# First attention: the mask moves from TensorE to VectorE, and the softmax subtraction from VectorE to GpSimd

## The reference

```python
xn = (x - mu) * jax.lax.rsqrt(var + LN_EPS) * ln_gamma + ln_beta
q = xn @ Wq
kv = context @ Wkv
dots = jnp.einsum('bhnd,bhmd->bhnm', q, k) * scale
dots = jnp.where(mask, dots, -jnp.inf)
attn = jax.nn.softmax(dots, axis=-1)
out = jnp.einsum('bhnm,bhmd->bhnd', attn, v)
return out @ Wo + bo
```

## Time and profile before

| | us |
|---|---|
| median of three runs | 2427.84 |
| span of the profiled execution | 2424.7 |
| TensorE busy | 2252.3 (93%) |
| VectorE busy | 1825.4 (75%) |
| ScalarE busy | 1492.7 (62%) |
| GpSimd busy | 517.2 (21%) |

### The profile page before, as it was taken

The page is one execution under the profiler, slowest core; times in us unless marked ns, Lnnn a source line. Parts: engine busy times, 40 slices in busy tenths (PEclk is TensorE's granted clock), DMA queues, the critical chain, the costliest instruction groups (busy, mean ns, idle before and its releaser), DMA issues.

```text
span 2424.7 us, 49203 instructions
## 1 busy us (share of the span) xinstructions
PE 2252.3 (93%) x14859; PEld 1942.3 (80%) x14861; DVE 1825.4 (75%) x4361; ACT 1492.7 (62%) x3090; POOL 517.2 (21%) x734
## 2 busy tenths in 40 slices
PE   7899999999899899995468999999997999979998
PEld 6788888888788788883147888888886788879998
DVE  3677777787966688887984877888878666865666
ACT  6455555556454677776886666666663654637666
POOL 2022221322212122121001111111101442421334
PEclk8999999999999999998579999999999999979999
DMA  8444544445300444440015455555452000115455
GB/s 216 115 129 127 141 132 135 131 122 145 95 16 8 127 128 128 135 125 27 0 37 152 135 142 149 144 138 144 131 139 72 1 1 1 39 41 146 140 141 159
DMA packets 461643, 256.56 MB, mean 106 GB/s; under 512 B 25664, under 2 KB 442332, under 8 KB 461532
## 3 DMA queue, kind: packets, MB, share of 16 engines
q1 hardware_dynamic: 461532, 255.27, 38.1%
HBM read 150.10 MB, written 105.12 MB: 105 GB/s over the span
## 4 chain that ended last, share of the span: by engine, by line
PE 79%; DVE 9%; ACT 5%; issue 4%; ACTq 0%; DMA 0%; POOL 0%; DVEq 0%; POOLq 0%
PE ps_o L906 13%; PE ps_s L890 12%; PE ps_p L87 7%; PE ps_p L89 7%; PE ps_p L88 7%; PE ps_t L879 6%; PE ps_o L1415 3%; PE ps_t L1415 2%; PE ps_s L3052 2%; PE ps_t L3070 2%; PE ps_o L3070 2%; PE ps_s L87 2%; PE ps_s L88 1%; PE ps_s L89 1%; DVE f_rng L1879 1%
## 5 line engine op out<-in xcount | busy, mean ns | idle before, releaser
L906 PEld LDWEIGHTS ps_o<-a_val,a_pt 128*128 128x128 f32 (+2 forms) x3200 | 412.5, 192 | 33.5 <-issue 7.6
L890 PE MATMUL ps_s<-a_keys,a_zt 128*128 128x308 f32 (+1 forms) x1024 | 416.8, 491 | 15.7 <-ACT a_keys L1025 9.8
L906 PE MATMUL ps_o<-a_val,a_pt 128*128 128x128 f32 (+2 forms) x3200 | 423.0, 275 | 5.3 <-ACT a_pt L1062 3.6
L1171 DVE TENSOR_REDUCE a_sm<-a_e 128x16 f32<-128x1232 f32 (+1 forms) x192 | 234.4, 1221 | 230.4 <-ACT a_e L1070 230.0
L1034 ACT ACTIVATE a_stage<-ps_p 128x512 f32<-128x512 f32 (+1 forms) x370 | 220.9, 597 | 287.7 <-PE ps_p L89 285.5
L1025 ACT ACTIVATE a_keys<-ps_p 128x308 f32<-128x308 f32 x603 | 257.5, 427 | 102.8 <-PE ps_p L89 102.3
L1062 ACT ACTIVATE a_pt<-ps_t 128x512 f32<-128x512 f32 (+1 forms) x448 | 225.3, 505 | 150.3 <-PE ps_t L879 149.9
L1156 DVE TENSOR_REDUCE a_mx<-ps_s 128x6 f32<-128x462 f32 (+1 forms) x512 | 256.5, 549 | 45.6 <-PE ps_s L890 28.5
L879 PE MATMUL ps_t<-ident,a_e 128*128 128x128 f32 (+1 forms) x1600 | 262.0, 276 | 28.1 <-DVE a_e L1179 25.8
L87 PE MATMUL ps_p<-ct_hi,a_mt_hi 96*128 (+1 forms) x603 | 258.9, 429 | 0.0
L1164 DVE TENSOR_TENSOR a_e<-ps_s,a_mx 128x462 f32<-128x462 f32 (+1 forms) x512 | 253.9, 546 | 0.0
(11 more groups left out here) (436 smaller groups left out, 4602.8 us busy)
## 6 DMA issues: line engine op xcount, KB each, us to landing
a_vals<-a_stage SPq DMA_DIRECT2D x160, 512.0 KB, 3.5
a_val<-a_vals SPq DMA_DIRECT2D x128, 576.0 KB
f_w<-in_L_ffn_W_dram SPq DMA_DIRECT2D x129, 256.0 KB, 2.7
a_vals<-a_stage SPq DMA_DIRECT2D x40, 416.0 KB
a_val<-a_vals SPq DMA_DIRECT2D x64, 256.0 KB
a_val<-a_vals SPq DMA_DIRECT2D x128, 40.0 KB
x<-in_x_dram SPq DMA_DIRECT2D x8, 512.0 KB, 7.0
out_dram<-x SPq DMA_DIRECT2D x7, 512.0 KB, 6.1
```

What stands on the lines that cost most here:

```text
L890: mm = eng.matmul(o, zt, keys[:, h0:h0 + nh, :], start=True, stop=not self.masked)
L906: mm = eng.matmul(c.ps_o[:, (i % 2) * P:(i % 2 + 1) * P], self.pt[0:r, n, :], self.val[0:r, i % 2, n, :], start=(n == 0), stop=(n == self. ...
L1171: eng.tensor_reduce(self.sm[:, :], e, AX.X, ALU.add).then_inc(st.sem, 1)
```

## The change

- TensorE no longer multiplies the mask in: 192 matmuls (three per tile) go, as does the rounded identity. Its wait for a free score bank is now on `scores_masked`.
- VectorE empties each score bank by adding the mask on the way to SBUF, and then takes the maxima from SBUF, in the order add 0, add 1, max 0, add 2, max 1, max 2. `mask_add` shrinks to one copy of 77 columns that the addition repeats over the heads. In the `found` iterations add 0 and max 0 come before `normalise`.
- GpSimd subtracts the maxima, bank by bank, SBUF to SBUF, and signals `shifted`. `mx` gets two halves.
- GpSimd's other work of this phase is reordered behind the subtractions: per iteration first the three subtractions of tile t+2, then, by position in the group, the bias addition, `next_stats.pool`, or the window copies and `ln.pool`. The window copies lose their wait for `probs_ready`.

```diff
     def scores(self, eng, t, b, zt, keys, first=False):
-            eng.wait_ge(self.shifted.sem, self.shifted.at(self.NB * (t - 1) + b + 1))
-        mm = eng.matmul(o, zt, keys[:, h0:h0 + nh, :], start=True, stop=not self.masked)
-        if self.masked:
-            mask = self.mask_add[:, 0:nh, :].rearrange("p h k -> p (h k)")
-            mm = eng.matmul(o, self.ident_r[:, :], mask, start=False, stop=True)
-        mm.then_inc(self.scores_ready.sem, 1)
+            eng.wait_ge(self.scores_read.sem, self.scores_read.at(self.NB * (t - 1) + b + 1))
+        eng.matmul(c.ps_s[:, b, 0:nh * KEYS], zt, keys[:, h0:h0 + nh, :], start=True, stop=True)\
+           .then_inc(self.scores_ready.sem, 1)
...
+    def masked_maxima(self, eng, t, par, banks):
+        def maximum(b):
+            heads, _, dest = self.bank_of(t, par, b)
+            eng.wait_ge(self.scores_masked.sem, self.scores_masked.at(self.NB * t + b + 1))
+            eng.tensor_reduce(self.mx[:, par, heads], dest, AX.X, ALU.max).then_inc(self.max_ready.sem, 1)
+        for b in banks:
+            _, src, dest = self.bank_of(t, par, b)
+            mask = self.mask_add[:, :].unsqueeze(1).broadcast_to([P, self.banks[b], KEYS])
+            eng.wait_ge(self.scores_ready.sem, self.scores_ready.at(self.NB * t + b + 1))
+            eng.tensor_tensor(dest, src, mask, ALU.add).then_inc(self.scores_masked.sem, 1)
+            if b - 1 in banks:
+                maximum(b - 1)
+        if banks:
+            maximum(banks[-1])
...
     def shift(self, eng, t, par, found=0):
+        if self.masked:
+            self.masked_maxima(eng, t, par, range(found, self.NB))
+            return
...
+    def shift_masked(self, eng, t, par):
+        for b in range(self.NB):
+            heads, _, dest = self.bank_of(t, par, b)
+            eng.wait_ge(self.max_ready.sem, self.max_ready.at(self.NB * t + b + 1))
+            eng.tensor_tensor(dest, dest, bc(self.mx[:, par, heads], KEYS), ALU.subtract)\
+               .then_inc(self.shifted.sem, 1)
...
+    def gpsimd_masked(self, eng, v_last):
+        self.shift_masked(eng, 0, 0)
+        self.shift_masked(eng, 1, 1)
+        for t in range(BATCH):
+            g, k = t // GT, t % GT
+            if t + 2 < BATCH:
+                self.shift_masked(eng, t + 2, k % 2)
+            if k == 1 and g + 1 < GROUPS:
+                self.ln.pool_bias(eng, g + 1)
+            elif k == 2 and g >= 1:
+                self.next_stats.pool(eng, g - 1)
+            elif k == 3:
+                w = t // self.WIN
+                if g % 2 == 1 and w + 2 < self.WINDOWS:
+                    eng.wait_ge(self.proj_done.sem, self.proj_done.at(self.use(w, v_last) + 1))
+                    self.copy_window(eng, w + 2)
+                if g + 2 < GROUPS:
+                    self.ln.pool(eng, g + 2)
+        self.next_stats.pool(eng, GROUPS - 1)
```

More of the change, by code:

```diff
@@ L631, in __init__ @@
             self.mask_u8 = sb(ctx, n("mask_u8"), [P, KEYS], mybir.dt.uint8)
-            self.mask_add = sb(ctx, n("mask_add"), [P, self.banks[0], KEYS], F32R)
-            self.ident_r = sb(ctx, n("ident_r"), [P, P], F32R)
+            self.mask_add = sb(ctx, n("mask_add"), [P, KEYS], F32)
             self.some_key = sb(ctx, n("some_key"), [P, 2], F32)
@@ L638, in __init__ @@
         self.val = sb(ctx, n("val"), [P, 2, self.chunks, P], F32)
-        self.mx = sb(ctx, n("mx"), [P, H], F32)
+        self.mx = sb(ctx, n("mx"), [P, 2, H], F32)
         self.sm = sb(ctx, n("sm"), [P, H], F32)
@@ L672, in __init__ @@
         self.lo_done = cl("split_lo", 4 * self.pairs)
-        self.mask_ready = cl("mask_ready", 5) if self.masked else None
+        self.mask_ready = cl("mask_ready", 4) if self.masked else None
         self.ln = TailLayerNorm(core, known, self.bias) if known else LayerNorm(core, twice, self.bias)
@@ L688, in __init__ @@
         self.shifted = cl("shifted", self.NB * T)
+        self.scores_masked = cl("scores_masked", self.NB * T) if self.masked else None
+        self.scores_read = self.scores_masked if self.masked else self.shifted
         self.exp_ready = cl("exp_ready", T)
@@ L971, in tensor @@
         eng.wait_ge(self.proj_copied.sem, self.proj_copied.at(self.first))
-        if self.masked:
-            eng.wait_ge(self.mask_ready.sem, self.mask_ready.at(5))
         for k in range(2):
@@ L1155, in maxima @@
             eng.wait_ge(self.scores_ready.sem, self.scores_ready.at(self.NB * t + b + 1))
-            eng.tensor_reduce(self.mx[:, heads], src, AX.X, ALU.max).then_inc(self.max_ready.sem, 1)
+            eng.tensor_reduce(self.mx[:, par, heads], src, AX.X, ALU.max).then_inc(self.max_ready.sem, 1)
+    def masked_maxima(self, eng, t, par, banks):
[12 more added lines that the diff above has]
+            maximum(banks[-1])
     def shift(self, eng, t, par, found=0):
+        if self.masked:
+            self.masked_maxima(eng, t, par, range(found, self.NB))
+            return
         self.maxima(eng, t, par, range(found, self.NB))
@@ L1163, in shift @@
             eng.wait_ge(self.max_ready.sem, self.max_ready.at(self.NB * t + b + 1))
-            eng.tensor_tensor(dest, src, bc(self.mx[:, heads], KEYS), ALU.subtract).then_inc(self.shifted.sem, 1)
+            eng.tensor_tensor(dest, src, bc(self.mx[:, par, heads], KEYS), ALU.subtract)\
+               .then_inc(self.shifted.sem, 1)
[4 more added lines that the diff above has]
+            eng.tensor_tensor(dest, dest, bc(self.mx[:, par, heads], KEYS), ALU.subtract)\
+               .then_inc(self.shifted.sem, 1)
     def normalise(self, eng, t, par):
@@ L1204, in vector @@
             m = self.mask_ready
-            for h in range(self.banks[0]):
-                ins = eng.tensor_scalar(self.mask_add[:, h, :], self.mask_u8[:, :], -1.0, 1e30, ALU.add, ALU.mult)
-            ins.then_inc(m.sem, 1)
+            eng.tensor_scalar(self.mask_add[:, :], self.mask_u8[:, :], -1.0, 1e30, ALU.add, ALU.mult)\
+               .then_inc(m.sem, 1)
             eng.tensor_reduce(self.some_key[:, 0:1], self.mask_u8[:, :], AX.X, ALU.add).then_inc(m.sem, 1)
@@ L1213, in vector @@
                .then_inc(m.sem, 1)
-            eng.tensor_copy(self.ident_r[:, :], c.ident[:, :]).then_inc(m.sem, 1)
-            eng.wait_ge(m.sem, m.at(5))
+            eng.wait_ge(m.sem, m.at(4))
         if not self.setup:
@@ L1243, in body @@
                 found = int(left <= 1 and not (last and k >= 2) and (last or self.heads == 16 and k >= 2))
-                self.maxima(eng, t + 2, k % 2, range(found))
+                (self.masked_maxima if self.masked else self.maxima)(eng, t + 2, k % 2, range(found))
                 if more:
@@ L1285, in gpsimd @@
             self.quant.over_partitions(eng, 0)
+        if self.masked:
+            self.ln.pool(eng, 1)
         eng.wait_ge(self.proj_done.sem, self.proj_done.at(self.vuses))
@@ L1290, in gpsimd @@
         v_last = max(place for mine in self.plan for kind, _, place in mine if kind == "v")
+        if self.masked:
+            self.gpsimd_masked(eng, v_last)
+            return
         def groups(w, more):
```

1 line of the change is left out of this document (removed).

## The result

The changed kernel takes 2413.67 us (median of 4 runs, 2413.41 to 2415.6) against 2428.64 for the kernel before (4 runs beside it). The ratio is 0.994, 95% interval 0.9926 to 0.9954: 0.6% faster, about 15 us. In a second comparison of the same two kernels it was 0.9961 (0.9948 to 0.9975). The forecast was 2452, slower by 1.0%, range 2427 to 2480; both its side and its range missed.

A forecast was written before the change was run, and what follows sets the result against it. TensorE bounded the kernel at 9.55 us per tile; afterwards the softmax ring would, at 9.76. Terms +11.8, +3.3, +2.3, -1.1, +4.6, +3.7 gave +24.6 on 2427.8: 2452 us, 1.0% slower, range 2427 to 2480.

The forecast's parts named there:

- the third term of the loop: GpSimd's three subtractions of the maxima per tile, priced from additions with two operands at 3.10 us.
- the loop: Softmax ring through VectorE, GpSimd and ScalarE from tile to tile: 9.76 us after the change, the new bound.
- the steady term: 55 tiles of the first attention, each slowed from 9.545 to 9.76 us: +11.8 us.
- the end: Last tiles of the first attention, where TensorE is light and the longer ring shows: +4.6 and +3.7 us.
- Rival 1: Cheap repeated operand: three subtractions under 2.7 us, TensorE stays the bound at 8.96 to 9.0 per tile: 2396; chance 0.12.
- rival 2: GpSimd somewhat cheaper, three subtractions near 2.75 us, ring 9.4: 2430, no change; chance 0.12.
- The loop of 7.8: Softmax ring in the kernel before: 7.8 us per tile, under TensorE's 9.55 and under 8.96 without the mask.
- Rival 4: VectorE's additions too are held by GpSimd, +1.1 us per tile, +60 to 70: 2518; chance 0.03.
- The start: Two tiles' masks no longer stand in front of the first sum: -1.1 us.
- The queue: GpSimd's other work between subtractions: window copies and layer-norm chain together run about 0.55 late in six iterations, +3.3 us.
- Rival 3: GpSimd falls behind its queue, small chains held by products (+18) or 0.1 more per subtraction (+19): 2471; chance 0.14.
- rival 5: TensorE's pauses cost it granted clock; no size given; chance 0.02.

The follow-up runs named there:

- experiment 3: Changed kernel plus six timed GpSimd instructions on a spare buffer, before the first subtractions: 462-column subtraction 960 ns with repeated value, 1191 with full operand.
- experiment 2: Changed kernel with one extra 231-column GpSimd subtraction per tile, so that the subtractions cost what was predicted: 2445.9 us, ratio 1.0072 to the kernel before.
- experiment 6: Changed kernel with the first bank's mask addition and maxima ahead of the sum in every tile (the early bank): 2400.3 us, ratio 0.9885 to the kernel before.
- experiment 7: One value projection moved from second to seventh tile of eight: changed kernel 2411.8 us, kernel before 2428.4, changed kernel with early first bank 2401.6.
- experiment 1: Kernel before without the mask's matmul, scores left unmasked: 2394.0 us, ratio 0.9864 to the kernel before.
- 6 (control): Kernel before with the first bank's maxima found ahead of the sum in every tile: 2426.2 us, ratio 0.9997 to the kernel before.
- experiment 4: Changed kernel with the three subtractions moved from GpSimd back to VectorE: 2438.3 us, ratio 1.0037 to the kernel before.
- experiment 8: Changed kernel with GpSimd's two window copies ahead of the subtractions of their tile: 2420.1 us, ratio 0.9966 to the kernel before.

## Why the prediction was wrong, point by point

**The step that failed** is the third term of the loop, "GpSimd, three subtractions", taken at 3.10 us and measured at 2.54. I fitted a line through 4 and 512 columns, which is right for full operands (experiment 3), and wrote that the repeated form "is not shown"; then I took the upper neighbour "same instruction, same number of streams". The repeat over 77 neighbours makes it 1.67 ns per column instead of 2.12. The bias, the repeated operand that I had read, repeats in the other direction and gave no hint. Put 2.54 into the working of the forecast and the loop is 9.20, the steady term 55 x (9.20 - 9.545) = -19.0, the end 2.9 + 2.3 instead of 4.6 + 3.7, the other terms as they stood: -9.3, 2418.5. The one mis-sized term turns +24.6 into -9.3, and experiment 2 shows the reverse on the chip. That the corrected sum comes so near is in part luck: it has even tiles of 9.20, 73.6 us for eight, where the trace has 74.0 made of tiles from 9.03 to 9.91. The loop's remaining 0.13 (9.07 instead of 9.20) were handovers that I had rounded up to 0.1 each: they took 0.08, 0.07 and 0.03.

**The second failure** was in the rivals. Rival 1 set its threshold at 2.7 us and named 8.96 to 9.0 per tile below it, 2396. The subtractions came in at 2.54, below the threshold, and the time is 2414. By the prediction's own sum 2.7 is only where the change stops costing time (24.6 us over some 60 tiles are 0.41 less than 3.10); TensorE at 8.96 needs the three under 3.10 - 0.80 = 2.30, and at 2.54 the loop is 9.20. And 8.96 is itself a mean over eight tiles. Against single tiles of 7.72 and 8.35 a loop of 9.05 is the bound still, and that costs 1.33 + 0.70 us per eight (experiments 6 and 7). For 2396 the loop has to be under 7.8, as in experiment 1. In the kernel before, show TensorE busy all the time, so its own time for each tile could be had from the distances of its sums less the mask.

**The bounds and chances.** Both ends, 1.6 and 6.9 us, held the true 2.54, but rivals 1 and 2 together had 0.24 (rival 2, at 2.75, was the nearest), though the sign of the result hung on where between 1.6 and 3.1 an unseen form would lie. The range ended at 2427 although a price between the two rows gave every time from 2396 upwards.

**What held.**
- TensorE as the bound before, and 0.55 us per tile for the mask: experiment 1, 2394 where -30 was worked out. The loop of 7.8 had slack against TensorE's pace: experiments 6 (control) and 7.
- The loop as new limit, and each microsecond of GpSimd in it one for one: experiments 2 and 6.
- Additions with the mask in SBUF are not held by GpSimd: 630 and 468 ns for 462 and 308 columns, 629 and 467 in experiment 4, where GpSimd subtracts nothing. Rival 4 is out. `z` is held: four took 1.72 us at 307.61, 1.09 beside no subtraction (experiment 4); VectorE had the slack.
- The end: +8.3 forecast, +5.4 measured (tiles 56 to 63 in 60.53 us instead of 55.15), with the smaller price in it; at the predicted price 63.75, +8.6. The start: -1.1 forecast, -1.7 in the profiled executions, inside what varies between kernels.
- The queue: copies and chain together run over. The subtractions of tile 26 start only at 306.19, directly behind the chain's last step, and that interval of subtractions is 9.43 (from 296.76) instead of 9.07: 0.36 where 0.55 was said.
- The product held one small step of a chain for 1.2 to 1.4 us, as read in the earlier trace rows. Rival 3 found no more than that: the other chains fit.
- Clock: 1.00 in the long stretch as before, so rival 5 is out there. In the last seven tiles it is not: a granted clock of 0.94 with TensorE busy for 49.56 of 60.53 us, where the kernel before had 1.00 with 50.82 of 55.15. What that costs was not separated; with the predicted price the end came out at +8.6 for +8.3 with no term for the clock.

**What was missing**: the window copies. In the kernel before they start 3.6 behind the sum of tile 23 (296.01 against 292.38), now behind the next tile's subtractions, 7.7 behind the sum of tile 24 (299.24 against 291.51), and TensorE waits 1.25 us for them in six windows. I had priced the copies' effect on the subtractions, not the subtractions' effect on the copies. It happened to cost little net (experiment 8).

**Where the gain went.** Phase before to after: 589.4 - 579.1 = 10.3 us won. TensorE's relief was 589.4 - 556.8 = 32.6. Of the 22.3 that were given back, the two short tiles account for about 2.0 x 7 = 14 and the last seven tiles for 60.5 - 54.5 = 6; the rest, some 2, is mostly in the tiles beside the window copies (9.40 for 9.13). The early bank recovers 14.7.

## What to carry to other kernels

Compare a loop with each tile of the engine that paces the kernel, not with its mean: where work is dealt unevenly, the short tiles lose their advantage first, and a loop has to get under the shortest one before the full gain shows. Moving work to an idle engine is worth the length that it has inside the loop, so start part of it before the loop's critical stretch; here an early first bank gave more of the phase (14.7 us) than the change itself (10.3). And where an operand's form is not in the trace, the forecast's range has to reach to both neighbours; an operand that repeats over neighbours and one that repeats over blocks are two forms.

## What the runs showed of the hardware

- A GpSimd subtraction whose second operand is a value repeated over 77 neighbours is faster than one with a full operand: 960 against 1191 ns for 462 columns; a block repeated four times is not faster (1297 against 1288 for 512). Each form was timed once (experiment 3); the first is 961 in the mean of 112 too. The Trainium skill, "GPSIMD Engine Reference", section 3.1, has 2.6 cycles per element for two inputs, which at its 1.2 GHz is an estimate of 2.17 ns: full operands agree (2.15), the repeated one (1.67 from 961 and 704 ns) is below it.
- A VectorE subtraction of two SBUF operands beside a GpSimd subtraction took 964 instead of 470 ns, GpSimd's own stayed at 965 in the mean. A VectorE product of two SBUF operands took 2.41 instead of 1.44 us beside a GpSimd copy. VectorE's additions of PSUM and SBUF (630 ns for 462 columns) and its maxima from SBUF (0.63 us) kept their lengths.
